# Queries and keys from the token-major product, transposed on TensorE, in place of three feature-major products

## The chip, the cores and the metric

The kernel runs on one core of a Trainium2 chip. The metric is the device time of one execution, in microseconds (us). The engines: TensorE (PE: matmuls and transposes, PEld its weight loads), VectorE (DVE), ScalarE (ACT), GpSimd (POOL), SyncE (SP, which issues DMAs).

## The reference

16 sequences ("groups") of 512 tokens with 128 features, fp32. Each is normalised; a causal linear attention with 32 channels and a decay, and a mixture of four experts with top-2 routing are computed of it and added to x.

```python
xn = _layernorm(x)
# attention, C = 32
q_w = basis @ q_coeffs.T                     # also k_w, v_w, o_w
queries, keys, values = xn @ q_w, xn @ k_w, xn @ v_w
scores = einsum('btc,bsc->bts', queries, keys)
diff = pos[None, :] - pos[:, None]
scores = scores * decay ** max(diff - 1, 0) * (diff > 0)
attn = (einsum('bts,bsc->btc', scores, values) @ o_w.T) * out_scale
# experts, top 2 of 4 by softmax of the logits
e0 = silu(xn @ w1) * (xn @ w3) @ w2
e1 = gelu(folded(xn) @ c1 + b) @ c2 + b
e2: syn -> attn -> layernorm -> relu FFN -> layernorm -> gen
e3 = gelu(xn @ ml_w1 + b) @ ml_w2 + b
out = x + attn + sum(weight * expert)
```

## The kernel before

**Products.** Most products are done as three float32r matmuls of high and low parts: high x high, low x high, high x low (`xh`, `xl` for the input, `WH`, `WL` for the weights). They are feature-major: weights stand, 512 tokens move, the result is features x tokens. The first product of a group, though, is token-major: for each of 4 tiles of 128 tokens, `xh`/`xl` stand and `TH`/`TL` move (lines 1146 to 1148). Its 196 columns are 128 for expert 2, 4 router logits, 32 of k and 32 of v.

**Order.** Everything is written out by hand, with semaphores. Each engine has a function `turn(g, first, last)`, called for group 0 and 1, for 2 to 13 in a loop over pairs, and for 14 and 15; a turn also holds leftovers of the group before. `UNITS` lists 24 products in the order in which TensorE fills the four PSUM banks `S0` to `S3` in turn: `tok0` to `tok3`, the first gate (`a0`, `b0`), four products of expert 3 (`c0` to `c3`), state (`st`), scores (`sc`), gate 1, and so on. A bank may be filled again when its reader has released it.

**A group on TensorE:** transposes of the last group's `u` into `ATT` (L1246); the token product; q and k, feature-major (L1155 to L1157) into `qk_bank`, which is `ATT` under another name and holds q, q, k, k in four times 32 partitions; gate 0 (`three`, L1133 to L1135); `c0` to `c3`; the state product of `kd` and `kv` (L1168); transposes of the normed `n1` (L1173); scores (L1179); gate 1; experts 1 and 2 of the group before; `pr` and `qd` into `ATT` (L1191, L1194); `f1`; attention's output (L1207 to L1209), which waits for `found_low`; gates 2 and 3; `e3`, `f2`, `m0`, `m1`, expert 0 (L1059).

**VectorE:** `u` statistics (L786); `pl` out of the token banks (L845), each behind the ScalarE copy of the same bank (`kv_taken`), which releases the bank; statistics; low part of Q (L856); gate 0's two products (L818, L822); low part of K (L861); expert 0's mixing; `qd` (L871), which is q, three times over on 96 partitions, times the decay table `reach`; `pr` (L811), the masked scores; `h2l` (L875); gate 1; expert 1's mixing; five routing steps; `foundl` (L716), the low part of what attention found; routing; and so on.

**ScalarE:** `kv` copies (L573); Q (L578: 96 partitions, q, q, k); tanh of gate 0 (L567); K twice (L580, L581); `kd` (L585); four Gelus out of `c0` to `c3` (L588), each releasing its bank; state (L590); `h2` (L592) and `h2h` (L595); tanh of gate 1; `hid3h`; `foundh` (L601).

**GpSimd** takes the roots and norms (`n1`, L454) and low parts of the hidden layers.

Setup folds weights: `qkv` is one product of 160 columns (q, q, k, k, v), which ScalarE and VectorE split into `WH`/`WL` (columns `qk`) and `TH`/`TL`.

Of the kernel before, what the change touches and what calls it, by code (L numbers as in the profile page):

```python
# [18 lines left out]
ALU = mybir.AluOpType  # L19
# [3 lines left out]
P = 128  # L23
GROUPS = 16
T = 512
NT = T // P
PAIRS = GROUPS // 2
C = 32
E = 4
I = 512  # L30
# [31 lines left out]
SPLIT, _at = {}, 0  # L62
for _name, _width in (("w1", I), ("w3", I), ("ml", I), ("f1", 2 * P), ("f2", 2 * P), ("w2", I), ("me", 2 * P), ("qk", 4 * C)):
    SPLIT[_name] = _at
    _at += _width
# [7 lines left out]
LOGW = P + E  # L73
TOKW = LOGW + 2 * C


B = 32
BEHIND = NT - 1
# [54 lines left out]
def build(nc: bass.Bass, x: bass.AP, weights: bass.AP, vecs: bass.AP, rows: bass.AP, out: bass.AP):  # L133
    with ExitStack() as ctx:
        def sb(name, shape, dt=F32):
            return ctx.enter_context(nc.sbuf_tensor(name, shape, dt))

        def sem(name):
            return ctx.enter_context(nc.semaphore(name))
# [19 lines left out]
        mask = sb("mask", [P, P])  # L159
        reach = sb("reach", [BEHIND * C, BEHIND * P])  # L160
        depth = sb("depth", [P, 2])
# [11 lines left out]
        xl = [sb(f"xl{k}", [P, T], F32R) for k in range(2)]  # L173
        kv = sb("kv", [P, NT, 2 * C])
        kd = sb("kd", [P, BEHIND, C])
# [88 lines left out]
        qk_ready = sem("qk_ready")  # L264
        qk_high = sem("qk_high")
        qk_split = sem("qk_split")
        kv_taken = sem("kv_taken")
# [81 lines left out]
        def _(sp):  # L349
# [20 lines left out]
            for n in range(BEHIND):  # L370
                sp.dma_start(reach[n * C:(n + 1) * C, :], bass.AP(source, start - (P - 1) - n * P,
                                                                  [diagonals.ap[0], [0, C], [1, BEHIND * P]])) \
                    .then_inc(mask_loaded, DMA_INC)
# [132 lines left out]
        def _(act):  # L506
# [14 lines left out]
            def high_weights(n):  # L521

                first_col, name, width = WEIGHT_SPLITS[n]
                act.wait_ge(w_loaded[LOAD_OF[name]], DMA_INC)
                src = w(name, 0, width)
                act.copy(WH[:, first_col:first_col + width], src).then_inc(split_high, 1)
# [13 lines left out]
            qkv = prod("qkv", cols=5 * C)  # L540
            at = SPLIT["qk"]
            act.copy(WH[:, at:at + 2 * C], qkv[:, 0:2 * C])
            act.copy(WH[:, at + 2 * C:at + 4 * C], qkv[:, C:3 * C])
            act.copy(TH[:, LOGW:TOKW], qkv[:, 3 * C:5 * C]).then_inc(fold_high, 1)
            act.copy(TH[:, 0:P], prod("ce")).then_inc(fold_high, 1)
# [13 lines left out]
            def turn(g, first, last):  # L559
# [11 lines left out]
                for t in range(NT):  # L571
                    tok, _ = unit(f"tok{t}")
                    act.copy(kv[:, t, :], tok[:, LOGW:TOKW]).then_inc(kv_taken, 1)  # L573
                if first:
                    for n in range(FIRST_SPLITS, len(WEIGHT_SPLITS)):
                        high_weights(n)
                act.wait_ge(qk_ready, g.count(1, 1))
                act.copy(Q[:, :], qk_bank[0:3 * C, :]).then_inc(qk_high, 1)  # L578
                half_gate(0)
                act.copy(K[0:C, :], qk_bank[3 * C:4 * C, :])  # L580
                act.copy(K[C:2 * C, :], qk_bank[3 * C:4 * C, :]).then_inc(qk_high, 1)  # L581
                if first:
                    act.wait_ge(depth_loaded, DMA_INC)
                act.wait_ge(kv_taken, g.count(NT, NT))
                act.mul(kd[:, :, :], kv[:, 1:NT, 0:C], depth[:, 0:1]).then_inc(kd_ready, 1)  # L585
                for j in range(4):
# [40 lines left out]
        def _(dve):  # L627
# [34 lines left out]
            n = 1  # L662
# [16 lines left out]
            def took(ins):  # L679

                ins.then_inc(setup_took, 1)
                dve.wait_ge(setup_took, taken[0])

            dve.tensor_tensor(tokb[:, P:P + E], row("router_b"), row("balancer"), ALU.add)
            product("qkv")
            qkv, at = prod("qkv", cols=5 * C), SPLIT["qk"]
            dve.wait_ge(fold_high, 1)
            dve.tensor_tensor(WL[:, at:at + 2 * C], qkv[:, 0:2 * C], WH[:, at:at + 2 * C], ALU.subtract)
            dve.tensor_tensor(WL[:, at + 2 * C:at + 4 * C], qkv[:, C:3 * C], WH[:, at + 2 * C:at + 4 * C], ALU.subtract)
            took(dve.tensor_tensor(TL[:, LOGW:TOKW], qkv[:, 3 * C:5 * C], TH[:, LOGW:TOKW], ALU.subtract))  # L690
            product("ce")
# [110 lines left out]
            def turn(g, first, last):  # L802
# [49 lines left out]
                for t in range(NT):  # L852
                    ins = dve.bn_aggr(mv["c"][:, t, :], stats["c"][:, t, :])
                ins.then_inc(c_stats, 1)
                dve.wait_ge(qk_high, g.count(2, 1))
                dve.tensor_tensor(Q[C:2 * C, :], qk_bank[C:2 * C, :], Q[C:2 * C, :], ALU.subtract)  # L856
                silu(0)
                if not first:
# [10 lines left out]
                if first:  # L869
                    dve.wait_ge(mask_loaded, (1 + BEHIND) * DMA_INC)  # L870
                dve.tensor_tensor(qd[:, :], qk_bank[0:BEHIND * C, 0:BEHIND * P], reach[:, :], ALU.mult) \  # L871
                    .then_inc(qd_ready, 1)
# [113 lines left out]
        def _(pe):  # L986
# [136 lines left out]
            def turn(g, first, last):  # L1123
# [26 lines left out]
                if first:  # L1150
                    fold_first()
                if not first:
                    pe.wait_ge(u_read, g.prev().count(1, 1))
                wh, wl = (m[:, SPLIT["qk"]:SPLIT["qk"] + 4 * C] for m in (WH, WL))
                pe.matmul(qk_bank, wh, h, start=True, stop=False)  # L1155
                pe.matmul(qk_bank, wh, l, start=False, stop=False)
                pe.matmul(qk_bank, wl, h, start=False, stop=True).then_inc(qk_ready, 1)  # L1157
                if first:
                    pe.wait_ge(split_low, 1)
                gates(0)  # L1160
                if first:
                    pe.wait_ge(split_low, 2)
# [4 lines left out]
                for n in range(BEHIND):  # L1167
                    ins = pe.matmul(bank[n * C:(n + 1) * C, 0:C], kd[:, n, :], kv[:, n + 1, C:2 * C],  # L1168
                                    start=True, stop=True)
# [20 lines left out]
                for t in range(NT):  # L1190
                    ins = pe.matmul(ATT[t * C:(t + 1) * C, 0, :], kv[:, t, C:2 * C], pr[:, t, :],  # L1191
                                    start=True, stop=(t == NT - 1))
# [121 lines left out]
```

## Time and profile before

| | |
|---|---|
| runs | 451.05, 451.26, 454.0 us; median 451.26 |
| span of the profiled execution | 449.1 us |
| TensorE | 438.6 us busy (98%) |
| VectorE | 402.5 us (90%) |
| ScalarE | 271.4 us (60%) |
| GpSimd | 245.8 us (55%) |
| TensorE clock | 1.00 in the periods looked at |

The profile is of one execution and gives its span, from the first to the last instruction; what lies around it is not in it. A busy share is an average over the span. In a timeline each row has start, duration, engine, line, operation and the tiles out<-in; a bracket at the end has the engine's idle time before it and what ended it. A matmul's record lasts longer than the step to the next one, since they are pipelined: the step between starts is what TensorE's time is made of.

### The profile page before, as it was taken

Reading aid. Unit: us, or ns where it says so; the run is one execution under the profiler, and the core shown is the slowest. Engines: PE = TensorE matmul, PEld = TensorE weight load, DVE = VectorE, ACT = ScalarE, POOL = GpSimd, SP = SyncE. Lnnn points to the kernel's source line nnn. Section 1 sums busy time; section 2 is a strip of 40 time slices with the busy share of each in tenths; the row PEclk is TensorE's granted clock in tenths of the full one; section 3 lists DMA queues with packets and bytes.
Section 4 is the critical chain, followed back from the end, with each engine's and each line's share of the span. In section 5 each row is a group of like instructions: output and inputs, shape, how many; then the busy total and the mean of one; then the engine's idle time right before and its main releaser. Section 6 shows DMA issues by size and latency. Waiting matters only on the chain.

```text
span 449.1 us, 9603 instructions
## 1 busy us (share of the span) xinstructions
PE 438.6 (98%) x2804; PEld 371.8 (83%) x2804; DVE 402.5 (90%) x1344; ACT 271.4 (60%) x535; POOL 245.8 (55%) x366
## 2 busy tenths in 40 slices
PE   4999999999999999999999999999999999999997
PEld 3778888788888888888888988888888888888886
DVE  4887989989899898989989899898989989898897
ACT  4965838557384764838556484755838566483841
POOL 3893727557273664727466272664727466372451
PEclk9999999999999999999999999999999999999999
DMA  7522123032130412223032130413123031220201
GB/s 261 38 72 72 25 63 78 26 93 47 51 70 23 105 35 70 47 70 70 23 93 47 55 62 23 113 27 89 27 70 70 23 99 41 58 58 16 58 0 48
DMA packets 86484, 27.18 MB, mean 61 GB/s; under 512 B 64993, under 2 KB 82113, under 8 KB 86465
## 3 DMA queue, kind: packets, MB, share of 16 engines
q1 hardware_dynamic: 86176, 26.94, 25.0%
q8 instruction: 9, 0.15, 0.1%
q14 instruction: 11, 0.08, 0.1%
q10 hardware_dynamic: 288, 0.01, 0.0%
HBM read 14.66 MB, written 12.06 MB: 60 GB/s over the span
## 4 chain that ended last, share of the span: by engine, by line
PE 94%; DVE 3%; DMA 1%; issue 0%; DVEq 0%; ACT 0%; SPq 0%
PE S L1133 14%; PE S L1135 13%; PE S L1134 13%; PE EX L1059 12%; PE EX L1079 6%; PE S L1223 3%; PE S L1218 3%; PE S L1219 3%; PE EX L1087 3%; PE TR L1173 2%; PE S L1231 2%; PE S L1230 2%; PE S L1229 2%; PE S L1148 2%; PE S L1147 2%; PE S L1146 2%
## 5 line engine op out<-in xcount | busy, mean ns | idle before, releaser
L486 POOL TENSOR_TENSOR hid3l<-hid,hid3h 128x512 fp32r<-128x512 f32 x64 | 80.3, 1287 | 29.3 <-ACT hid3h L599 29.3
L1133 PE MATMUL S<-xh,WH 128*128 128x512 f32 x224 | 90.4, 403 | 0.0
L1135 PE MATMUL S<-xh,WL 128*128 128x512 f32 x224 | 88.4, 394 | 0.0
L1134 PE MATMUL S<-xl,WH 128*128 128x512 f32 x224 | 88.1, 393 | 0.0
L444 POOL TENSOR_TENSOR veps_x<-mv_x,eps 128x4 f32<-128x4 f32 x16 | 3.2, 200 | 111.7 <-DVE mv_x L643 111.7
L1059 PEld LDWEIGHTS EX<-scaled,hid 128*128 128x128 f32 x480 | 55.9, 192 | 1.2
L1059 PE MATMUL EX<-scaled,hid 128*128 128x128 f32 x480 | 56.0, 275 | 0.0
L1133 PEld LDWEIGHTS S<-xh,WH 128*128 128x128 f32 x224 | 42.2, 188 | 14.1 <-DVE hid L822 3.1
L1135 PEld LDWEIGHTS S<-xh,WL 128*128 128x128 f32 x224 | 42.1, 188 | 9.9
L573 ACT COPY kv<-S 128x64 f32<-128x64 f32 x64 | 13.6, 213 | 60.3 <-PE S L1148 54.6
L1134 PEld LDWEIGHTS S<-xl,WH 128*128 128x128 f32 x224 | 42.3, 189 | 8.0
L822 DVE TENSOR_TENSOR hid<-gate,S 128x512 f32<-128x512 f32 x64 | 44.0, 688 | 4.2
L490 POOL TENSOR_TENSOR hidl<-hid,hidh 128x512 fp32r<-128x512 f32 x32 | 40.9, 1300 | 11.0 <-ACT hidh L609 11.0
L818 DVE SCALAR_TENSOR_TENSOR gate<-th,S 128x512 f32<-128x512 f32 x64 | 43.8, 684 | 1.8
L567 ACT ACTIVATE th<-S 128x512 f32<-128x512 f32 x64 | 38.1, 595 | 8.8 <-PE S L1135 6.9
L588 ACT ACTIVATE hid<-S,VEC 128x512 f32<-128x512 f32 x64 | 38.8, 690 | 0.4
L752 DVE SCALAR_TENSOR_TENSOR OUT<-EX,coef,OUT 128x128 f32<-128x128 f32 x124 | 34.8, 344 | 0.6 <-PE EX L1069 0.2
L599 ACT CAST hid3h<-hid 128x512 fp32r<-128x512 f32 x64 | 34.6, 615 | 0.0
L621 ACT ACTIVATE hid<-S,me_b 128x512 f32<-128x512 f32 x32 | 22.0, 687 | 19.2 <-PE S L1135 19.1
L519 ACT CAST xh<-TR 128x512 fp32r<-128x512 f32 x16 | 9.4, 588 | 37.6 <-DVE TR L800 37.4
L1079 PEld LDWEIGHTS EX<-W,hid 128*128 128x128 f32 x240 | 29.1, 191 | 1.3
L454 POOL TENSOR_SCALAR n<-pl,negmean_c,rstd_c 128x128 f32<-128x128 f32 x64 | 27.8, 451 | 2.8 <-issue 2.8
(201 smaller groups left out, 1066.4 us busy)
## 6 DMA issues: line engine op xcount, KB each, us to landing
X<-x SPq DMA_DIRECT2D x16, 256.0 KB, 2.8
turning<-xn SPq DMA_DIRECT2D x15, 256.0 KB, 2.6
xb<-turning SPq DMA_DIRECT2D x60, 64.0 KB, 2.6
turning<-e3T SPq DMA_DIRECT2D x15, 256.0 KB, 2.4
e3b<-turning SPq DMA_DIRECT2D x60, 64.0 KB, 2.6
out<-OUT SPq DMA_DIRECT2D x15, 256.0 KB, 2.4
W<-weights SPq DMA_DIRECT2D x1, 768.0 KB, 8.2
W<-weights SPq DMA_DIRECT2D x1, 512.0 KB, 5.8
```

The lines of the kernel that those rows point to most:

```text
L486: pool.tensor_tensor(hid3l[:, j, :], hid[3][:, j, :], hid3h[:, j, :], ALU.subtract) \
L490: pool.tensor_tensor(hidl[:, j, :], hid[2][:, j, :], hidh[:, j, :], ALU.subtract) \
L567: act.activation(th[:, j, :], a[:, :], ACT.Tanh, scale=0.5).then_inc(th_ready, 1)
L588: act.activation(hid[3][:, j, :], c[:, :], ACT.Gelu, bias=vec(f"ml_b1{j}")).then_inc(free, 1)
L752: ins = dve.scalar_tensor_tensor(out=OUT[g.par][:, t, :], in0=(src or EX[EX_BANK[e]])[:, t, :], scalar=coef[g.par][:, t, e:e + 1], in1=OUT ...
L818: dve.scalar_tensor_tensor(out=gate[:, j, :], in0=th[:, j, :], scalar=1.0, in1=a[:, :], op0=ALU.add, op1=ALU.mult).then_inc(a_free, 1)
L822: dve.tensor_tensor(hid[0][:, j, :], gate[:, j, :], b[:, :], ALU.mult).then_inc(b_free, 1)
L1059: ins = pe.matmul(EX[EX_BANK[0]][:, t, :], hid[0][:, j, t * P:(t + 1) * P], scaled[:, j * P:(j + 1) * P], start=(j == 0), stop=(j == 3))
L1079: ins = pe.matmul(EX[EX_BANK[1]][:, t, :], hid[1][:, j, t * P:(t + 1) * P], w("me_c2w", j * P, P), start=(j == 0), stop=(j == 1))
L1133: pe.matmul(bank[:, :], wh, hi, start=True, stop=False)
L1134: pe.matmul(bank[:, :], wh, lo, start=False, stop=False)
L1135: pe.matmul(bank[:, :], wl, hi, start=False, stop=True).then_inc(unit_ready, 1)
```

## The change

q and k come out of the token-major product as well. Its columns become 228: q, k and v, 32 each, behind the 132. ScalarE's copy takes all three and writes each twice, so that `kv[:, t]` has q, q, k, k, v, v (192 columns). TensorE transposes the first 128 of them, four tiles, into `qk_bank`, which then holds q, q, k, k on its partitions as before. The three feature-major matmuls and their weights in `WH`/`WL` go. On TensorE gate 0 stands in front of the transposes. On ScalarE the tanh of gate 0 stands in front, Q is copied for 64 partitions, K in one copy of 64, and the third part of Q is now q again, in a copy of its own (`q_again`). On VectorE gate 0 stands ahead of the low part of Q, and `qd` is two instructions, on 64 and on 32 partitions, as `qk_bank` has q only twice; `reach` is split likewise. Lines of the changed kernel are 2 to 6 further down.

```diff
-for ... ("me", 2 * P), ("qk", 4 * C)):
+for ... ("me", 2 * P)):
-TOKW = LOGW + 2 * C
+TOKW = LOGW + 3 * C
-        reach = sb("reach", [BEHIND * C, BEHIND * P])
+        reach = sb("reach", [2 * C, BEHIND * P])
+        reach_far = sb("reach_far", [C, BEHIND * P])
-        kv = sb("kv", [P, NT, 2 * C])
+        kv = sb("kv", [P, NT, 3, 2, C])
...
# ScalarE, setup
-            act.copy(WH[:, at:at + 2 * C], qkv[:, 0:2 * C])
-            act.copy(WH[:, at + 2 * C:at + 4 * C], qkv[:, C:3 * C])
-            act.copy(TH[:, LOGW:TOKW], qkv[:, 3 * C:5 * C]).then_inc(fold_high, 1)
+            act.copy(TH[:, LOGW:LOGW + 2 * C], qkv[:, C:3 * C])
+            act.copy(TH[:, LOGW + 2 * C:TOKW], qkv[:, 4 * C:5 * C]).then_inc(fold_high, 1)
# ScalarE, turn
-                    act.copy(kv[:, t, :], tok[:, LOGW:TOKW]).then_inc(kv_taken, 1)
+                    both = tok[:, LOGW:TOKW].rearrange("p (a c) -> p a c", a=3).unsqueeze(2).broadcast_to([P, 3, 2, C])
+                    act.copy(kv[:, t, :, :, :], both).then_inc(kv_taken, 1)
...
+                half_gate(0)
                 act.wait_ge(qk_ready, g.count(1, 1))
-                act.copy(Q[:, :], qk_bank[0:3 * C, :]).then_inc(qk_high, 1)
-                half_gate(0)
-                act.copy(K[0:C, :], qk_bank[3 * C:4 * C, :])
-                act.copy(K[C:2 * C, :], qk_bank[3 * C:4 * C, :]).then_inc(qk_high, 1)
+                act.copy(Q[0:2 * C, :], qk_bank[0:2 * C, :]).then_inc(qk_high, 1)
+                act.copy(K[0:2 * C, :], qk_bank[2 * C:4 * C, :]).then_inc(qk_high, 1)
+                act.copy(Q[2 * C:3 * C, :], qk_bank[0:C, :]).then_inc(q_again, 1)
# VectorE, turn
+                silu(0)
                 dve.wait_ge(qk_high, g.count(2, 1))
                 dve.tensor_tensor(Q[C:2 * C, :], qk_bank[C:2 * C, :], Q[C:2 * C, :], ALU.subtract)
-                silu(0)
...
-                dve.tensor_tensor(qd[:, :], qk_bank[0:BEHIND * C, 0:BEHIND * P], reach[:, :], ALU.mult) \
+                dve.wait_ge(q_again, g.count(1, 1))
+                dve.tensor_tensor(qd[0:2 * C, :], qk_bank[0:2 * C, 0:BEHIND * P], reach[:, :], ALU.mult)
+                dve.tensor_tensor(qd[2 * C:3 * C, :], qk_bank[0:C, 0:BEHIND * P], reach_far[:, :], ALU.mult) \
                     .then_inc(qd_ready, 1)
# TensorE, turn
+                gates(0)
                 if not first:
                     pe.wait_ge(u_read, g.prev().count(1, 1))
-                wh, wl = (m[:, SPLIT["qk"]:SPLIT["qk"] + 4 * C] for m in (WH, WL))
-                pe.matmul(qk_bank, wh, h, start=True, stop=False)
-                pe.matmul(qk_bank, wh, l, start=False, stop=False)
-                pe.matmul(qk_bank, wl, h, start=False, stop=True).then_inc(qk_ready, 1)
-                gates(0)
+                for t in range(NT):
+                    pe.wait_ge(kv_taken, g.count(NT, t + 1))
+                    ins = pe.transpose(qk_bank[:, t * P:(t + 1) * P],
+                                       kv[:, t, 0:2, :, :].rearrange("p a b c -> p (a b c)"), ident[:, :])
+                ins.then_inc(qk_ready, 1)
...
                 pe.wait_ge(qk_split, g.count(1, 1))
+                pe.wait_ge(q_again, g.count(1, 1))
```

On TensorE, at the start of group 1, before, from the last matmul of the token product to the first of `c0` (`S` are the four banks):

```order
L1148 MATMUL S<-TH,xl 128x196
L1155 MATMUL ATT<-xh,WH 128x512 [waits u_read]
L1156 MATMUL ATT<-xl,WH 128x512
L1157 MATMUL ATT<-xh,WL 128x512
L1133 MATMUL S<-xh,WH 128x512 [waits released0]
L1134 MATMUL S<-xl,WH 128x512
L1135 MATMUL S<-xh,WL 128x512
L1133 MATMUL S<-xh,WH 128x512 [waits released1]
L1134 MATMUL S<-xl,WH 128x512
L1135 MATMUL S<-xh,WL 128x512
L1133 MATMUL S<-xh,WH 128x512 [waits released2]
```

The same place after:

```order
L1152 MATMUL S<-TH,xl 128x228
L1137 MATMUL S<-xh,WH 128x512 [waits released0]
L1138 MATMUL S<-xl,WH 128x512
L1139 MATMUL S<-xh,WL 128x512
L1137 MATMUL S<-xh,WH 128x512 [waits released1]
L1138 MATMUL S<-xl,WH 128x512
L1139 MATMUL S<-xh,WL 128x512
L1163 MATMUL ATT<-ident,kv 128x128 [waits kv_taken,u_read]
L1163 MATMUL ATT<-ident,kv 128x128 [waits kv_taken] x3
L1137 MATMUL S<-xh,WH 128x512 [waits released2]
```

Gate 0 has moved directly behind the token product, and four transposes stand behind it, in front of `c0`.

On VectorE in the same group, before, from the statistics of `pl` to the low part of `h2`:

```order
L853 BN_AGGR mv_c<-stats_c 128x2 x4
L856 TENSOR_TENSOR Q<-ATT,Q 32x512 [waits qk_high]
L818 SCALAR_TENSOR_TENSOR gate<-th,S 128x512 [waits th_ready]
L822 TENSOR_TENSOR hid<-gate,S 128x512 [waits released0,unit_ready]
L792 BN_AGGR mv_u<-stats_u 128x2 x4
L861 TENSOR_TENSOR K<-ATT,K 32x512 [waits qk_high]
...
L871 TENSOR_TENSOR qd<-ATT,reach 96x384
L811 TENSOR_TENSOR pr<-S,mask 128x512 [waits unit_ready]
L875 TENSOR_TENSOR h2l<-h,h2h 128x512 [waits h2_high]
```

The same place after:

```order
L855 BN_AGGR mv_c<-stats_c 128x2 x4
L820 SCALAR_TENSOR_TENSOR gate<-th,S 128x512 [waits th_ready]
L824 TENSOR_TENSOR hid<-gate,S 128x512 [waits released0,unit_ready]
L859 TENSOR_TENSOR Q<-ATT,Q 32x512 [waits qk_high]
L794 BN_AGGR mv_u<-stats_u 128x2 x4
L863 TENSOR_TENSOR K<-ATT,K 32x512 [waits qk_high]
...
L874 TENSOR_TENSOR qd<-ATT,reach 64x384 [waits q_again]
L875 TENSOR_TENSOR qd<-ATT,reach_far 32x384
L813 TENSOR_TENSOR pr<-S,mask 128x512 [waits unit_ready]
L879 TENSOR_TENSOR h2l<-h,h2h 128x512 [waits h2_high]
```

The gate's two instructions have moved ahead of the low part of Q, and `qd` has become two.

## Rows read from the trace of the kernel before

**Rows 1.** The page: span; engines' busy time, share and instructions.

```profile
span 449.1 us, 9603 instructions
PE 438.6 (98%) x2804; PEld 371.8 (83%) x2804; DVE 402.5 (90%) x1344; ACT 271.4 (60%) x535; POOL 245.8 (55%) x366
```

**Rows 2.** Busy time by engine in one period: PE, PEld, DVE, ACT, POOL; TensorE clock.

```profile
200.64:227.47 26.83, 26.83 (x174) 22.73 (x173) 24.68 (x82) 16.46 (x32) 14.94 (x23) 1.00 0.24 58
```

**Rows 3.** Timeline of TensorE, 202 to 228: start, duration, engine, line, operation.

```profile
202.40 0.42 PE L1155 MATMUL ATT<-xh,WH 128*128 128x512 f32 x1
...
203.13 0.40 PE L1133 MATMUL S<-xh,WH 128*128 128x512 f32 x1
...
205.91 0.43 PE L1133 MATMUL S<-xh,WH 128*128 128x512 f32 x1
...
207.64 0.66 PE L1173 MATMUL TR<-ident,n 128*128 128x128 f32 x4
...
223.90 3.73 PE L1059 MATMUL EX<-scaled,hid 128*128 128x128 f32 x32
227.47 0.60 PE L1246 MATMUL ATT<-ident,u 128*128 128x128 f32 x4
```

**Rows 4.** Timeline of VectorE, 202 to 229.

```profile
202.09 0.28 DVE L845 TENSOR_TENSOR pl<-S,tokb 128x132 f32<-128x132 f32 x1
...
202.85 0.29 DVE L845 TENSOR_TENSOR pl<-S,tokb 128x132 f32<-128x132 f32 x1
...
204.41 0.68 DVE L856 TENSOR_TENSOR Q<-ATT,Q 32x512 fp32r<-32x512 f32 x1
205.10 0.69 DVE L818 SCALAR_TENSOR_TENSOR gate<-th,S 128x512 f32<-128x512 f32 x1
...
208.78 0.54 DVE L871 TENSOR_TENSOR qd<-ATT,reach 96x384 f32<-96x384 f32 x1
209.25 0.68 DVE L811 TENSOR_TENSOR pr<-S,mask 128x512 f32<-128x512 f32 x1
210.09 0.69 DVE L875 TENSOR_TENSOR h2l<-h,h2h 128x512 fp32r<-128x512 f32 x1 [0.17 <-ACT h2h L595]
...
214.31 0.29 DVE L716 TENSOR_TENSOR foundl<-ATT,foundh 128x128 fp32r<-128x128 f32 x1
...
228.11 0.89 DVE L786 BATCH_NORM_STATS2 stats_u<-ATT 128x6 f32<-128x128 f32 x4 [0.94 <-PE ATT L1246]
```

**Rows 5.** TensorE's matmuls and weight loads (PEld) at 214.6.

```profile
214.58 0.39 PE L1135 MATMUL S<-h2h,WL 128*128 128x512 f32 x1
214.82 0.39 PE L1207 MATMUL ATT<-backh,foundh 128*128 128x512 f32 x1
...
214.65 0.19 PEld L1207 LDWEIGHTS ATT<-backh,foundh 128*128 128x128 f32 x1
```

**Rows 6.** Group 0: VectorE and TensorE at the attention's output.

```profile
26.51 0.28 DVE L716 TENSOR_TENSOR foundl<-ATT,foundh 128x128 fp32r<-128x128 f32 x1
...
26.94 0.47 PE L1207 MATMUL ATT<-backh,foundh 128*128 128x512 f32 x1 [0.26 <-DVE foundl L716]
```

**Rows 7.** The transposes of `n`: durations (ns) min/median/max, first and last start.

```profile
L1173 PE MATMUL TR<-ident,n x64: 272/273/329, 20.6 to 422.8; 128*128 128x128 f32 x64
```

**Rows 8.** Timeline of ScalarE, 202 to 214.

```profile
202.60 0.21 ACT L573 COPY kv<-S 128x64 f32<-128x64 f32 x1
...
204.64 0.58 ACT L580 CAST K<-ATT 32x512 fp32r<-32x512 f32 x1
...
205.84 0.38 ACT L585 ACTIVATE kd<-kv,depth 128x96 f32<-128x96 f32 x1
206.24 2.43 ACT L588 ACTIVATE hid<-S,VEC 128x512 f32<-128x512 f32 x4
...
209.44 0.62 ACT L595 CAST h2h<-h 128x512 fp32r<-128x512 f32 x1
...
213.44 0.27 ACT L601 CAST foundh<-ATT 128x128 fp32r<-128x128 f32 x1 [0.82 <-PE ATT L1194]
```

More of the change, by code:

```diff
@@ L62 @@
 SPLIT, _at = {}, 0
-for _name, _width in (("w1", I), ("w3", I), ("ml", I), ("f1", 2 * P), ("f2", 2 * P), ("w2", I), ("me", 2 * P), ("qk", 4 * C)):
+for _name, _width in (("w1", I), ("w3", I), ("ml", I), ("f1", 2 * P), ("f2", 2 * P), ("w2", I), ("me", 2 * P)):
     SPLIT[_name] = _at
@@ L265, in build @@
         qk_high = sem("qk_high")
+        q_again = sem("q_again")
         qk_split = sem("qk_split")
@@ L370, in _ @@
             for n in range(BEHIND):
-                sp.dma_start(reach[n * C:(n + 1) * C, :], bass.AP(source, start - (P - 1) - n * P,
-                                                                  [diagonals.ap[0], [0, C], [1, BEHIND * P]])) \
+                to = reach[n * C:(n + 1) * C, :] if n < 2 else reach_far[:, :]
+                sp.dma_start(to, bass.AP(source, start - (P - 1) - n * P,
+                                          [diagonals.ap[0], [0, C], [1, BEHIND * P]])) \
                     .then_inc(mask_loaded, DMA_INC)
@@ L540, in _ @@
             qkv = prod("qkv", cols=5 * C)
-            at = SPLIT["qk"]
-            act.copy(WH[:, at:at + 2 * C], qkv[:, 0:2 * C])
-            act.copy(WH[:, at + 2 * C:at + 4 * C], qkv[:, C:3 * C])
-            act.copy(TH[:, LOGW:TOKW], qkv[:, 3 * C:5 * C]).then_inc(fold_high, 1)
+            act.copy(TH[:, LOGW:LOGW + 2 * C], qkv[:, C:3 * C])
+            act.copy(TH[:, LOGW + 2 * C:TOKW], qkv[:, 4 * C:5 * C]).then_inc(fold_high, 1)
             act.copy(TH[:, 0:P], prod("ce")).then_inc(fold_high, 1)
@@ L584, in turn @@
                 act.wait_ge(kv_taken, g.count(NT, NT))
-                act.mul(kd[:, :, :], kv[:, 1:NT, 0:C], depth[:, 0:1]).then_inc(kd_ready, 1)
+                act.mul(kd[:, :, :], kv[:, 1:NT, 1, 0, :], depth[:, 0:1]).then_inc(kd_ready, 1)
                 for j in range(4):
@@ L685, in _ @@
             product("qkv")
-            qkv, at = prod("qkv", cols=5 * C), SPLIT["qk"]
+            qkv = prod("qkv", cols=5 * C)
             dve.wait_ge(fold_high, 1)
-            dve.tensor_tensor(WL[:, at:at + 2 * C], qkv[:, 0:2 * C], WH[:, at:at + 2 * C], ALU.subtract)
-            dve.tensor_tensor(WL[:, at + 2 * C:at + 4 * C], qkv[:, C:3 * C], WH[:, at + 2 * C:at + 4 * C], ALU.subtract)
-            took(dve.tensor_tensor(TL[:, LOGW:TOKW], qkv[:, 3 * C:5 * C], TH[:, LOGW:TOKW], ALU.subtract))
+            dve.tensor_tensor(TL[:, LOGW:LOGW + 2 * C], qkv[:, C:3 * C], TH[:, LOGW:LOGW + 2 * C], ALU.subtract)
+            took(dve.tensor_tensor(TL[:, LOGW + 2 * C:TOKW], qkv[:, 4 * C:5 * C], TH[:, LOGW + 2 * C:TOKW],
+                                   ALU.subtract))
             product("ce")
@@ L1151, in turn @@
                     fold_first()
-                if not first:
-                    pe.wait_ge(u_read, g.prev().count(1, 1))
-                wh, wl = (m[:, SPLIT["qk"]:SPLIT["qk"] + 4 * C] for m in (WH, WL))
-                pe.matmul(qk_bank, wh, h, start=True, stop=False)
-                pe.matmul(qk_bank, wh, l, start=False, stop=False)
-                pe.matmul(qk_bank, wl, h, start=False, stop=True).then_inc(qk_ready, 1)
                 if first:
@@ L1160, in turn @@
                 gates(0)
+                if not first:
+                    pe.wait_ge(u_read, g.prev().count(1, 1))
+                for t in range(NT):
[3 more added lines that the diff above has]
+                ins.then_inc(qk_ready, 1)
                 if first:
@@ L1167, in turn @@
                 for n in range(BEHIND):
-                    ins = pe.matmul(bank[n * C:(n + 1) * C, 0:C], kd[:, n, :], kv[:, n + 1, C:2 * C],
+                    ins = pe.matmul(bank[n * C:(n + 1) * C, 0:C], kd[:, n, :], kv[:, n + 1, 2, 0, :],
                                     start=True, stop=True)
@@ L1190, in turn @@
                 for t in range(NT):
-                    ins = pe.matmul(ATT[t * C:(t + 1) * C, 0, :], kv[:, t, C:2 * C], pr[:, t, :],
+                    ins = pe.matmul(ATT[t * C:(t + 1) * C, 0, :], kv[:, t, 2, 0, :], pr[:, t, :],
                                     start=True, stop=(t == NT - 1))
```

## The prediction

> **What bounds the kernel now.** I read the page first: TensorE is busy 98% of the span, VectorE 90% [rows 1]. The reader should not stop there, since a record that is busy says nothing of whether it could have started earlier. So I took one period, the stretch from one group's transposes of `u` (200.64) to the next one's (227.47): 26.83 us, no idleness on TensorE, its clock at 1.00 [rows 2]. Then I read each engine's timeline in it. The three feature-major matmuls of q and k take TensorE from 202.40 to 203.13, so 0.24 us each; the twelve that start from 203.13 on, up to 205.91, take 0.232 each [rows 3]. VectorE stands idle for 0.94 us until the `u` transposes are done, and from there to `foundl` it has one gap, 0.17 us, where `h2l` waits for ScalarE's `h2h` [rows 4]. `foundl` ends at 214.31 + 0.29 = 214.60. The weights of the matmul that waits for it are loaded at 214.65, a little behind the start of the matmul before it (214.58), which is where a load starts that waits for nothing; the matmul itself still starts on time at 214.82 [rows 5]. How much could be spared there is seen in group 0, where TensorE did stand idle for `foundl`: it ended at 26.51 + 0.28 = 26.79, the matmul started at 26.94, 0.15 us later [rows 6]. In the steady group 214.60 + 0.15 = 214.75, so the slack ahead of 214.82 is 0.07 us. So two chains make one period: VectorE with ScalarE from the end of the `u` transposes to `foundl`, and TensorE from there to the end of the next `u` transposes. What lengthens the first by more than 0.07 us is paid in every group, whatever TensorE saves in the meantime.
>
> **TensorE's own account.** Three matmuls of 512 columns go: 203.13 - 202.40 = 0.73 us [rows 3]. Four transposes of 128x128 come. The nearest are those of `n`: the record of four lasts 0.66 from 207.64, each one 0.27 [rows 3, 7], so the last starts 0.39 behind the first; with its own pitch of 0.13 at most that is 0.52, and with the 0.11 that 128 columns take elsewhere ((227.47 - 223.90) / 32 [rows 3]) 0.44. I take 0.44, as most rows have it. The token product goes from 196 to 228 columns, twelve times. Below: 228 columns at the rate of 512 would take 0.232 x 228 / 512 = 0.10, less than the 0.11 that 128 columns take anyway, so nothing. Above: by a line from 128 columns (0.11) to 512 (0.232), 32 x 0.00032 = 0.010 each, 0.12 in all. I take 0.04, near the flat end. TensorE's work shrinks by 0.73 - 0.44 - 0.04 = 0.25 us a group, 4.0 us over 16.
>
> The Trainium skill, "TensorE: Matmul & The Clock Gate", section on PE-mode transpose, gives about 275 ns for a 128x128 transpose in a kernel's context, mostly access latency. By that number as the cost of each in a row, four would take 1.1 us, and the 0.25 saved would be 0.41 lost. The trace has the same duration and decides against that reading: each record lasts 273 ns [rows 7], and they start 0.13 us apart with the clock at 1.00 [rows 2, 3].
>
> **VectorE's part.** (a) The `kv` copy writes 192 columns instead of 64. The fourth starts at 202.60 and lasts 0.21 [rows 8]; the fourth `pl` starts 0.04 behind its end, at 202.85 [rows 4]: VectorE waits for it. For 192 columns the bounds are 0.21 (if only what is read counts) and 0.62 (the 512 columns of `h2h`). `foundh`, 128 columns out of PSUM, takes 0.27, so 64 more columns cost 0.06 [rows 8]; twice that gives 0.33, I take 0.32. `pl` and all behind it come 0.11 + 0.04 (the token product) = 0.15 later. (b) The gate comes ahead of the Q subtraction: three instructions in another order, nothing. (c) `qd` becomes two instructions of 384 columns. If cost went by partitions this would be free (end: 0). But the Q subtraction on 32 partitions takes 0.68, `pr` on 128 partitions 0.68 [rows 4]. So each costs what the one did, from `qd` at 208.78 to `pr` at 209.25: 0.47 more. VectorE is free for `h2l` 0.62 later, less the 0.17 of idleness: 0.45.
>
> **ScalarE's part.** Q, tanh, K, K, `kd` becomes tanh, Q, K, Q again, `kd`, but Q now waits for transposes that stand behind the first gate. The first gate's matmul waits for the first `pl`, 202.09 + 0.28 = 202.37; from a release to the matmul it is 0.12 (gate ends 205.10 + 0.69 = 205.79, matmul at 205.91) [rows 3, 4]: 202.49. Six matmuls at 0.232: 203.88. From the first transpose's start to the last's 0.39, its record 0.27, a semaphore's 0.04: Q starts at 204.58. Three copies at 0.60 (K at 204.64, two of them, `kd` at 205.84) and `kd` 0.40: the first Gelu at 206.78 instead of 206.24 [rows 8]. From the Gelus ScalarE runs without a gap to the end of `h2h` (209.44 + 0.62), which so comes 0.54 later. That is more than VectorE's 0.45 and decides: `h2l`, and `foundl` with it, 0.54 late; less the slack of 0.07, TensorE's matmul on `foundh` starts 0.47 late.
>
> **Where TensorE's saving goes.** Queued behind the new waits on TensorE are the state product, the scores and gate 1; they need the banks of the first three Gelus, which come 0.54 late, so the 0.25 saved is waited away there, inside the 0.47 and not on top of it. Behind `foundl` TensorE runs on as before. VectorE, 0.54 late, still has its 0.94 us ahead of the next `u` statistics [rows 4], so nothing is added and nothing recovered.
>
> **The sum.** 15 groups x 0.47 = 7.05 us. In group 0 VectorE is the later one already (0.26 us of idleness at `foundl` [rows 6]), so the second `qd` counts in full: 0.5. Setup loses some copies and subtractions of 64 columns ahead of the first group; at most 0.2 us, and the wider `kv` copies of group 0 take it back: nothing. Its DMAs are as many as before, and SP's queue is the same. Span 449.1 [rows 1] + 7.5 = 456.6. The profile gives no other time of its execution than the span; the median of the runs, 451.26, stands 2.2 above it: 458.8 us, 1.7% more.
>
> **Rivals.** *TensorE's work decides.* For it: 98% busy. Against it: the 0.07 of slack. It needs a second `qd` at next to nothing and a ScalarE order that fits, so that `foundl` comes less than 0.07 late. It gives -4.0: 447.3, and with the flat ends (token product free) 446.6. 0.11, of it 0.05 faster by over 1%.
> *Only the second `qd` counts.* ScalarE is early enough, since Q's copy on fewer partitions is short, and the `kv` copy stays at 0.21: 0.47 + 0.04 - 0.17 - 0.07 = 0.27 a group, and 0.2 if the pitch is shorter; 3 to 4 us, 454.8, within 1%. 0.10.
> *The wide `kv` copy is dear.* It writes in four dimensions; `kd` in three blocks takes 0.38 for 96 columns [rows 8], so 0.46 may be true for 192. Then the four copies run one behind the other from 201.59 (three pitches of 0.34 ahead of 202.60), the last ends at 203.43 instead of 202.81, VectorE is at `h2l` 0.62 + 0.47 - 0.17 = 0.92 late: 0.85 a group, 13 us, 464. 0.08.
> *Transposes at their full 0.27 in a row.* 0.7 later through Q, Gelu and `h2h`: 1.1 a group, 17 us, 468. 0.03.
> The forecast has 0.68.
>
> **From this to the numbers.** A measurement of this kernel tells about 1% from no change. Slower by over 1%: 0.68 + 0.08 + 0.03 = 0.79; within: 0.10 + 0.06 = 0.16; faster: 0.05. The range goes down to 450, so that it holds the second rival and leaves out the first, and up to 463, for a copy somewhat dearer than 0.32; the forecast's own is 455.5 to 462 (0.28 to 0.7 a group).
>
> **What will show it.** Right, step by step: two `qd` of 0.54; `kv` copies near 0.32; the first Gelu 6.1 us behind the `u` transposes' start (206.78 less 200.64) and `h2l` waiting for `h2h`; the weights of the matmul on `foundh` 0.4 us behind the start of the matmul ahead, or TensorE idle for `foundl`; a period of 27.3 us with VectorE's wait for the `u` transposes still near 0.9. Wrong: a period under 26.9; a `kv` copy over 0.4; q and k transposes that start over 0.2 us apart; TensorE's longest wait at another matmul than that on `foundh`.

## The result, and the profile after

The changed kernel takes 456.86 us (median of 4 runs), the kernel before 451.15 beside it: a ratio of 1.0119, interval 1.0087 to 1.0151. The forecast was slower, 458.8 us in a range of 450 to 463; measured are +5.7 us instead of +7.5.

One thing on the kernels has to be put right first. The description ahead of the prediction says that `qk_bank` holds q, q, k, k before the change too, and that the copy on 96 partitions is q, q, k. In fact it holds q, q, q, k before, and the copy is q three times over; q, q, k, k is the changed kernel's order, which is why it needs a further copy of q and a second `qd`. No number of the prediction rests on this.

The page of the changed kernel (busy time, share, instructions), where TensorE is still busy 97%, answers to [rows 1]:

```profile
span 454.4 us, 9652 instructions
PE 440.7 (97%) x2820; PEld 372.0 (82%) x2820; DVE 409.2 (90%) x1359; ACT 276.6 (61%) x534; POOL 246.7 (54%) x366
```

The same period as in [rows 2], from one group's `u` transposes to the next (busy time of PE, PEld, DVE, ACT, POOL; clock):

```profile
202.82:229.99 27.17, 27.02 (x176) 22.78 (x174) 25.09 (x83) 16.77 (x32) 14.96 (x23) 1.00 0.24 57
```

27.17 us instead of 26.83, at the same clock. 0.34 in 15 groups is 5.1 of the 5.3 us by which the span grew. To compare instants with those before, take 2.18 us off: the `u` statistics start at 203.46 here and at 201.28 there.

TensorE's timeline, answering to [rows 3] and [rows 5]:

```profile
202.82 0.60 PE L1252 MATMUL ATT<-ident,u 128*128 128x128 f32 x4
...
203.37 0.28 PE L1151 MATMUL S<-TL,xh 128*128 128x228 f32 x1
...
204.48 0.28 PE L1152 MATMUL S<-TH,xl 128*128 128x228 f32 x1
204.60 0.50 PE L1137 MATMUL S<-xh,WH 128*128 128x512 f32 x1
...
206.11 0.60 PE L1163 MATMUL ATT<-ident,kv 128*128 128x128 f32 x4
206.46 0.48 PE L1137 MATMUL S<-xh,WH 128*128 128x512 f32 x1
...
216.87 0.40 PE L1139 MATMUL S<-h2h,WL 128*128 128x512 f32 x1
217.23 0.50 PE L1213 MATMUL ATT<-backh,foundh 128*128 128x512 f32 x1
217.57 0.40 PE L1214 MATMUL ATT<-backh,foundl 128*128 128x512 f32 x1
```

The work on TensorE did shrink: the four transposes take 0.35 us (206.11 to 206.46) and the 228 columns the same 0.11 as 196 (203.37 to 204.48 for ten steps). But between the matmul at 216.87 and the second of the attention's output (L1214) at 217.57 lie 0.70 us for two matmuls that took 0.47 before (214.58 to 215.05). VectorE's timeline says why, answering to [rows 4]:

```profile
203.46 0.89 DVE L788 BATCH_NORM_STATS2 stats_u<-ATT 128x6 f32<-128x128 f32 x4 [1.07 <-PE ATT L1252]
204.27 1.18 DVE L847 TENSOR_TENSOR pl<-S,tokb 128x132 f32<-128x132 f32 x4
...
206.30 0.38 DVE L855 BATCH_NORM_AGGREGATE mv_c<-stats_c 128x2 f32<-128x6 f32 x4
206.59 0.66 DVE L820 SCALAR_TENSOR_TENSOR gate<-th,S 128x512 f32<-128x512 f32 x1
...
210.94 0.54 DVE L874 TENSOR_TENSOR qd<-ATT,reach 64x384 f32<-64x384 f32 x1
211.49 0.55 DVE L875 TENSOR_TENSOR qd<-ATT,reach_far 32x384 f32<-32x384 f32 x1
212.07 0.69 DVE L813 TENSOR_TENSOR pr<-S,mask 128x512 f32<-128x512 f32 x1
212.68 0.68 DVE L879 TENSOR_TENSOR h2l<-h,h2h 128x512 fp32r<-128x512 f32 x1
...
216.88 0.29 DVE L718 TENSOR_TENSOR foundl<-ATT,foundh 128x128 fp32r<-128x128 f32 x1
```

`h2l` is 0.41 later than before (212.68 - 2.18 - 210.09), `foundl` 0.39. ScalarE, answering to [rows 8]:

```profile
206.74 0.58 ACT L581 CAST Q<-ATT 64x512 fp32r<-64x512 f32 x1 [0.54 <-PE ATT L1163]
207.35 0.59 ACT L582 CAST K<-ATT 64x512 fp32r<-64x512 f32 x1
207.96 0.57 ACT L583 CAST Q<-ATT 32x512 fp32r<-32x512 f32 x1
208.56 0.38 ACT L587 ACTIVATE kd<-kv,depth 128x96 f32<-128x96 f32 x1
208.84 2.41 ACT L590 ACTIVATE hid<-S,VEC 128x512 f32<-128x512 f32 x4
...
212.01 0.62 ACT L597 CAST h2h<-h 128x512 fp32r<-128x512 f32 x1
```

`h2h` ends at 212.63, VectorE comes out of `pr` at the same time, and `h2l` starts at 212.68 with no idleness: two engines arrive together. The waits (total, times, longest) have a line that they did not have before:

```profile
DVE stats_u L788 <- PE ATT L1252: 18.4, 15, 2.4
...
PEld ATT L1213 <- DVE foundl L718: 6.5, 15, 0.6
```

The weights of the matmul on `foundh` wait 0.43 us for `foundl` in each of 15 groups. In the program the one wait for `foundl` stands ahead of all three matmuls of that output, though only the second reads it; no run moved the wait. VectorE still idles ahead of the `u` statistics, 1.07 us, so it is not VectorE's total that is short: it is a chain of VectorE's and ScalarE's instructions from the `u` transposes to `foundl`.

### The profile page after: what moved, and what is told of

Its sections match the earlier page's. It is cut to its first block, busy times and chain, and to the rows that moved or that the text cites. A ratio compares the mean times of both kernels' runs of the same rounds, so it can differ in the third digit from the quotient of the medians.

```text
span 454.4 us, 9652 instructions
## 1 busy us (share of the span) xinstructions
PE 440.7 (97%) x2820; PEld 372.0 (82%) x2820; DVE 409.2 (90%) x1359; ACT 276.6 (61%) x534; POOL 246.7 (54%) x366
## 3 DMA queue, kind: packets, MB, share of 16 engines
q1 hardware_dynamic: 86176, 26.94, 24.7%
## 4 chain that ended last, share of the span: by engine, by line
PE 77%; DVE 10%; issue 5%; ACT 5%; DMA 1%; DVEq 1%; SPq 0%; ACTq 0%
PE EX L1063 12%; PE S L1137 10%; PE S L1138 9%; PE S L1139 9%; PE EX L1083 5%; PE S L1229 3%; PE S L1224 3%; PE S L1225 3%; PE EX L1091 2%; PE TR L1178 2%; DVE OUT L754 2%; PE ATT L1213 2%; PE S L1235 2%; PE S L1236 2%; PE S L1237 2%
## 5 line engine op out<-in xcount | busy, mean ns | idle before, releaser
L1137 PE MATMUL S<-xh,WH 128*128 128x512 f32 x224 | 92.4, 413 | 0.0
L575 ACT COPY kv<-S 128x192 f32<-128x192 f32 x64 | 20.4, 320 | 55.5 <-PE S L1152 54.8
L568 ACT ACTIVATE th<-S 128x512 f32<-128x512 f32 x64 | 38.2, 596 | 18.4 <-PE S L1139 18.4
L788 DVE BATCH_NORM_STATS2 stats_u<-ATT 128x6 f32<-128x128 f32 x64 | 14.3, 286 | 18.4 <-PE ATT L1252 18.4
```

Of the source, the lines that this page charges most:

```text
L1137: pe.matmul(bank[:, :], wh, hi, start=True, stop=False)
```

## The experiments

Two theories were open. A: that chain sets the period, and of its two halves (VectorE's, ScalarE's) the later one counts; besides it GpSimd's norm of `n` holds up gate 1. Against it: one edit alone is the cost (second `qd`, ScalarE's third copy, the order), or TensorE's work is.

**One instruction for `qd`.** The last third of `qd` is then k times the decay, so the far part of attention is left out.

```diff
-                dve.tensor_tensor(qd[0:2 * C, :], qk_bank[0:2 * C, 0:BEHIND * P], reach[:, :], ALU.mult)
-                dve.tensor_tensor(qd[2 * C:3 * C, :], qk_bank[0:C, 0:BEHIND * P], reach_far[:, :], ALU.mult) \
+                dve.tensor_tensor(qd[:, :], qk_bank[0:BEHIND * C, 0:BEHIND * P], reach[:, :], ALU.mult) \
```

> The changed kernel with qd as one instruction on 96 partitions (its last third is then k times the decay, so the attention's far part is not computed). Theory A (the chain from the u transposes over VectorE and ScalarE to foundl sets the period; in the changed kernel h2l starts at 212.68 both because VectorE is just free and because h2h has just ended): VectorE comes 0.66 us earlier to h2l but waits there for ScalarE; no gain, 455.5 to 457 us. Rival B (the second qd on VectorE is the whole cost): back to 451.5 us. Rival C (TensorE's own work costs): 456.9 us, with no new wait of VectorE at h2l.

Measured: 455.64 us, ratio 1.0097 (1.0069 to 1.0126). The waits of this run:

```profile
DVE h2l L877 <- ACT h2h L596: 8.7, 16, 0.6
PEld ATT L1211 <- DVE foundl L717: 6.5, 15, 0.5
```

VectorE saved 0.6 us a group and stood idle nearly as long for `h2h` (8.7 us in 16 waits); TensorE's wait for `foundl` is still 6.5 us. The period hardly moved: 27.16 (`u` statistics at 202.79 and 229.95). Of what it is below the changed kernel, about half lies ahead of the loop: the first `u` statistics start at 39.87 us in this trace and at 40.44 in the changed kernel's. Rival B falls.

**One instruction for Q.** The last third of Q is k, so one of the three terms of the scores is another one.

```diff
-                act.copy(Q[0:2 * C, :], qk_bank[0:2 * C, :]).then_inc(qk_high, 1)
+                act.copy(Q[:, :], qk_bank[0:3 * C, :]).then_inc(qk_high, 1)
-                act.copy(Q[2 * C:3 * C, :], qk_bank[0:C, :]).then_inc(q_again, 1)
```

> The changed kernel with Q copied in one ScalarE instruction on 96 partitions and no copy of q again (Q's last third is then k, so one term of the scores is not computed rightly). Theory A: ScalarE has h2h 0.6 us earlier, but VectorE is only free for h2l at the same time as now; no gain, 455.5 to 457 us. Rival D (ScalarE's order and third copy are the whole cost): -0.34 us a group, 451.5 us.

Measured: 457.43 us, ratio 1.0111 (1.0061 to 1.0160): no gain. Rival D falls too.

**Both.**

> Both edits together. Theory A: h2l and foundl come about 0.6 us earlier, TensorE no longer waits for foundl (0.23 us a group), but gate 1 stays where it is, since the last transpose of n waits for GpSimd's norm: 452 to 454 us. Rival E (TensorE's work sets the period once foundl is out of the way): 26.83 - 0.25 us a group, 447 us. Rivals B or D alone: the same as the one of the two single edits.

Measured: 451.68 us, ratio 1.0007 (0.9985 to 1.0029), 5.2 us below the changed kernel where the single edits gave 1.2 and nothing. By the periods, 4.1 of it comes from the loop (15 x 0.27). The sum of two edits that are worth nothing alone is the mark of two chains that end together. `foundl` is gone from the waits (but for group 0), and in its place stands GpSimd:

```profile
PEld TR L1173 <- POOL n L455: 4.3, 15, 0.3
```

The period is 26.90 (`u` statistics at 202.76 and 229.66), not the 26.58 that TensorE's work alone would give: rival E falls. The time itself was 0.3 below what theory A had given.

**The order back**, in the changed kernel: transposes ahead of gate 0 on TensorE, Q ahead of the tanh, low part of Q ahead of the gate.

```diff
+                for t in range(NT):
+                    pe.wait_ge(kv_taken, g.count(NT, t + 1))
...
                 gates(0)
-                for t in range(NT):
-                    pe.wait_ge(kv_taken, g.count(NT, t + 1))
```

> The changed kernel with the transposes of q and k in front of gate 0 again, on TensorE, ScalarE (Q ahead of the tanh) and VectorE (low part of Q ahead of the gate). Theory A: TensorE waits about 0.4 us for the last kv copy, ScalarE reaches the Gelus 0.5 us earlier, VectorE 0.13 later since the low part of Q stands in front of the gate; VectorE decides: 458 us (457 to 459). Rival F (gate first is what costs, by holding up Q on ScalarE): 451 to 453 us.

Measured: 458.89 us, ratio 1.0146 (1.0099 to 1.0192). On TensorE the transposes take 0.66 us (207.21 to 207.87) instead of 0.35, since the last waits for its `kv` copy:

```profile
207.21 0.90 PE L1160 MATMUL ATT<-ident,kv 128*128 128x128 f32 x4
207.87 0.49 PE L1137 MATMUL S<-xh,WH 128*128 128x512 f32 x1
...
207.78 0.14 PEld L1160 LDWEIGHTS ATT<-ident,kv 128*128 128x128 f32 x1 [0.19 <-ACT kv L575]
```

TensorE's wait for `foundl` grew from 6.5 to 7.9 us in all. Gate 0 in front does not cost here, it saves 2 us; 1.7 of them are the period, 27.28 instead of 27.17 in the middle groups.

**The order alone**, in the kernel before: gate 0 ahead of the three feature-major products, on all three engines.

```diff
+                gates(0)
                 pe.matmul(qk_bank, wh, h, start=True, stop=False)
                 pe.matmul(qk_bank, wh, l, start=False, stop=False)
                 pe.matmul(qk_bank, wl, h, start=False, stop=True).then_inc(qk_ready, 1)
-                gates(0)
```

> The kernel before with gate 0 in front of the three feature-major products, on TensorE, ScalarE and VectorE: the order alone. Theory A: Q's copy starts 1.4 us later and the tanh falls out between, so the first Gelu comes 0.7 to 0.8 us later, and with it h2h, h2l and foundl; less 0.07 of slack 0.65 a group: 460 to 462 us. Rival (the order is free, as GpSimd and TensorE have other limits): 450 to 452 us.

Measured: 461.79 us, ratio 1.0239 (1.0218 to 1.0261), with `h2l` waiting up to 1.0 us for ScalarE:

```profile
DVE h2l L875 <- ACT h2h L595: 15.6, 16, 1.0
```

The same order that saves 2 us in the changed kernel costs 10.6 in this one, where the products wait for no `kv` copy and Q is just later.

**Two instructions for `qd`**, in the kernel before, nothing else.

```diff
-                dve.tensor_tensor(qd[:, :], qk_bank[0:BEHIND * C, 0:BEHIND * P], reach[:, :], ALU.mult) \
+                dve.tensor_tensor(qd[0:2 * C, :], qk_bank[0:2 * C, 0:BEHIND * P], reach[0:2 * C, :], ALU.mult)
+                dve.tensor_tensor(qd[2 * C:3 * C, :], qk_bank[2 * C:3 * C, 0:BEHIND * P], reach[2 * C:3 * C, :], ALU.mult) \
```

> The kernel before with qd as two instructions, on 64 and on 32 partitions, nothing else: VectorE 0.66 us more up to pr (0.55 + 0.58 instead of 0.47, as in the changed kernel), less 0.17 of idleness and 0.07 of slack: 0.42 a group, 457 to 458 us. Rival (VectorE's 90% leave room for 0.5 us a group): 451 us.

Measured: 457.01 us, ratio 1.0126 (1.0109 to 1.0143). VectorE's timeline:

```profile
211.71 0.54 DVE L871 TENSOR_TENSOR qd<-ATT,reach 64x384 f32<-64x384 f32 x1
212.27 0.56 DVE L872 TENSOR_TENSOR qd<-ATT,reach 32x384 f32<-32x384 f32 x1
212.85 0.69 DVE L811 TENSOR_TENSOR pr<-S,mask 128x512 f32<-128x512 f32 x1
```

1.14 us from `qd` to `pr` instead of 0.47, and a period of 27.17 in the middle groups, the changed kernel's. This one instruction costs as much as the whole change.

**One product of three**, in the kernel before. The two products with low parts are left out, 0.47 us a group of TensorE's work, more than the change took.

```diff
-                pe.matmul(qk_bank, wh, h, start=True, stop=False)
-                pe.matmul(qk_bank, wh, l, start=False, stop=False)
-                pe.matmul(qk_bank, wl, h, start=False, stop=True).then_inc(qk_ready, 1)
+                pe.matmul(qk_bank, wh, h, start=True, stop=True).then_inc(qk_ready, 1)
```

> The kernel before with only the first of the three feature-major products of q and k (the low parts are left out): TensorE has 0.47 us a group less to do, more than the change took off it. Theory A: nothing of it reaches the period, since the last transpose of n waits for GpSimd's norm and foundl has 0.07 of slack: 450 to 451.2 us, TensorE's wait shows ahead of the transposes of n. Rival E (TensorE's work sets the time): 16 x 0.47 = 7.5 us less, 443.6 us.

Measured: 451.31 us, ratio 1.0011 (0.9993 to 1.0029). An engine that is busy 98% had 7.5 us taken off and the time did not move, not even by the little that theory A allowed. The idleness showed, but not where the expectation had it: the products `c2` waited for VectorE's gate.

```profile
PEld S L1133 <- DVE gate L818: 10.3, 16, 0.7
```

The longest was 0.2 in the kernel before. The first line here is the second matmul of `c2` in the kernel before (the first is the one at 205.91 [rows 3]); the others are the `u` transposes and the first two matmuls of `c2` in this run:

```profile
206.18 0.39 PE L1134 MATMUL S<-xl,WH 128*128 128x512 f32 x1
...
200.50 0.60 PE L1244 MATMUL ATT<-ident,u 128*128 128x128 f32 x4
...
205.71 0.50 PE L1133 MATMUL S<-xh,WH 128*128 128x512 f32 x1 [0.23 <-DVE gate L818]
206.04 0.39 PE L1134 MATMUL S<-xl,WH 128*128 128x512 f32 x1
```

From the `u` transposes to `c2`'s second matmul it is 5.54 us in both (206.18 - 200.64, 206.04 - 200.50). So in the kernel before `c2` was already held by gate 0, which ended at 205.79: it lost 0.04 there (205.91 to 206.18 is 0.27, not 0.23), while the matmuls around `foundl` kept their step of 0.23. GpSimd's norm of `n` is as tight:

```profile
206.13 1.74 POOL L454 TENSOR_SCALAR n<-pl,negmean_c,rstd_c 128x128 f32<-128x128 f32 x4 [0.17 <-issue]
...
207.64 0.42 PEld L1173 LDWEIGHTS TR<-ident,n 128*128 128x128 f32 x4
```

It ends at 207.87, and the last of the four loads, of 0.14, starts 0.05 later. Both hang on the same `pl` and statistics of VectorE.

**The wide `kv` copy**, in the kernel before: k and v written three times each.

```diff
-                    act.copy(kv[:, t, :], tok[:, LOGW:TOKW]).then_inc(kv_taken, 1)
+                    wide = tok[:, LOGW:TOKW].rearrange("p (a c) -> p a c", a=2).unsqueeze(2).broadcast_to([P, 2, 3, C])
+                    act.copy(kv[:, t, :, :, :], wide).then_inc(kv_taken, 1)
```

> The kernel before with the kv copy written three times over (192 columns, 0.32 us as in the changed kernel), nothing else. VectorE's fourth pl, the statistics and GpSimd's norm come 0.11 us later. Theory A: the h2l side hides it in its 0.17 us of idleness, the last transpose of n does not: 0.05 to 0.11 us a group, 452 to 453 us. Rival (a copy on an engine that is 60% busy costs nothing): 451.2 us.

Measured: 452.96 us, ratio 1.0040 (1.0022 to 1.0057); its period is 26.94 (`u` statistics at 201.82 and 228.76), 0.11 longer. 0.11 us of a copy, on an engine 60% busy, goes into the period in full, through `pl` and the statistics. The wait that grew is not the one that was expected. It is `c2`'s for gate 0; in the kernel before it was the second line:

```profile
PEld S L1134 <- DVE gate L819: 4.7, 15, 0.3
...
PEld S L1133 <- DVE gate L818: 3.1, 15, 0.2
```

GpSimd's norm comes 0.10 later as well and is again followed by the last load at once, so which of the two holds the period is not separated here.

**Moves that should cure it.** First `foundl` alone, from behind the fifth routing step to behind the second, in the changed kernel.

```diff
                 route(dve.tensor_tensor(same, other, mine, ALU.is_equal))
+                if not first:
+                    found_rest(g)
...
-                if not first:
-                    found_rest(g)
                 route(dve.tensor_reduce(rank, same, AX.X, ALU.add))
```

> The changed kernel with foundl moved up on VectorE, from behind the fifth routing step to behind the second (0.8 us earlier). Theory A: TensorE no longer waits for foundl (0.23 us a group); gate 1 stays bound by GpSimd's norm, which the wide kv copy has put 0.11 us later, so the period is 26.93: 453 us (452 to 454), like the two relieved edits together. Rival (a second wait takes its place behind foundl, or VectorE's later work moves with it): 455 to 457 us.

Measured: 453.59 us, ratio 1.0062 (1.0037 to 1.0086), period 26.89 (202.31 to 229.20), as expected. An instruction of 0.29 us, moved, gives back 3.3 of the 5.7 us. The period is that of the run with both edits (26.90), though the times differ by 1.9 us: what lies ahead of the loop differs from trace to trace, and the first `u` statistics start anywhere from 39.9 to 42.4 us in the fourteen.

Then also half of expert 1's products in front of the state product, for both kernels:

```diff
+                if not first:
+                    expert1(g.prev(), 0)    # tiles 0 and 1
                 pe.wait_ge(kd_ready, g.count(1, 1))
...
-                    expert1(g.prev())
+                    expert1(g.prev(), 1)    # tiles 2 and 3
```

> The same, and on TensorE half of expert 1's products of the group before (0.9 us) stand ahead of the state product and the transposes of n, as cover for GpSimd's norm. Theory A: both waits are covered now, and TensorE's own account decides at last: 26.33 to 26.6 us a group, 444 to 448 us. Rival (moving c_turned back moves h2, h2h and h2l back by as much, and the wait reappears at f1 or foundl): 451 to 453 us.

> The kernel before with the same two moves (foundl up, half of expert 1 ahead of the transposes of n). Theory A: TensorE's own account here is 26.58 to 26.75 us a group: 447 to 450 us, and 2 to 4 us above the changed kernel with the same moves, since the 0.25 us of TensorE that the change saves counts now. Rival: no gain, as both versions have another wait: 451 us, and the changed one not faster than it.

Measured: 453.64 us (1.0050; 1.0032 to 1.0067) for the changed kernel: no further gain. 455.68 us (1.0105; 1.0080 to 1.0130) for the one before, which is worse than without the moves. In the changed one TensorE now runs through to gate 3 without waiting, and then waits for VectorE's gate 2, which frees the bank of `e3`:

```profile
PEld S L1228 <- DVE gate L820: 7.2, 15, 0.6
```

The expectation's rival named the wrong place, theory A the wrong time. For the kernel before, the rival was right in its first half, no gain; the changed kernel is 2.0 us faster than it with the same moves, as theory A had it. TensorE waits at the same place there, 6.8 us, and the transposes of `n` come too late for ScalarE, so that `h2l` waits:

```profile
PEld S L1222 <- DVE gate L818: 6.8, 15, 0.5
...
ACT h L592 <- PE TR L1177: 5.8, 15, 0.4
DVE h2l L875 <- ACT h2h L595: 5.6, 15, 0.4
```

Last, the scaling of expert 2 (1.1 us on VectorE) also moved from ahead of gate 2 to behind it, in the changed kernel.

```diff
-                if not first:
-                    expert2_scale(g.prev())
...
                 silu(2)
+                if not first:
+                    expert2_scale(g.prev())
```

> The changed kernel with foundl up, half of expert 1 ahead of the transposes of n, and on VectorE the four instructions that scale expert 2 (1.1 us) moved from ahead of gate 2 to behind it. In the run with the first two moves TensorE's idleness had gone to the product e3, whose bank gate 2 frees (7.2 us in 15 waits, up to 0.6). Theory A (chain after chain in a stream on VectorE that is nearly full, each to be put behind what TensorE waits for): this wait goes too, the period is 26.4 to 26.65 us, 446 to 449 us, below both kernels. Rival (VectorE itself is now the bound, at about 25.7 us of work and 0.8 of wait for the u transposes a group, and yet another wait appears): 451 to 454 us.

Measured: 451.36 us, ratio 1.0003 (0.9981 to 1.0024). The wait for gate 2 is gone. The `u` transposes at 200.75 and 227.35 are 26.60 apart, but the periods on either side are 27.03 and 27.02, and the mean of 14 is 26.78 (26.84 in the kernel before):

```profile
DVE stats_u L788 <- PE ATT L1256: 3.5, 2, 2.4
...
PE S L1139 <- DVE pl L847: 1.6, 5, 0.6
```

VectorE's wait for the `u` transposes, 18.4 us in 15 groups in the changed kernel, is down to 3.5 in 2, and TensorE waits for `pl` instead. VectorE has hardly any reserve left, and gate 0, which the change put directly behind the token product, needs its `pl` first. The rival of this expectation was right. No version beat the kernel before.

## Why the prediction was right, and where its sizes were off

**The bound.** Right for the changed kernel: `foundl` sets its period, and not TensorE's work, as the run with `foundl` moved and the run with both edits show. Right also that TensorE's work does not set the time of the kernel before, which the run with one product of three shows. But what held that kernel was not `foundl`, which still had its slack. It was VectorE's gate 0 at `c2`, or GpSimd's norm just behind it. The prediction counted neither. It was lucky in that: the change itself puts gate 0 ahead of the low part of Q, so that it ends 0.72 earlier (206.59 + 0.66 - 2.18 = 205.07 instead of 205.79) and no longer counts, and the norm, 0.13 late, costs less than `foundl` does.

**TensorE's saving.** The prediction had 0.25 us a group. Its terms were off both ways: four transposes took 0.35 and not 0.44, and the wider token product nothing, but gate 0's first matmul, now directly behind that product, waits for the first `pl` (204.27 + 0.28, weights from 204.60). From the `u` transposes to the first matmul of `c0` it was 3.87 (204.51 - 200.64) and is 3.64 (206.46 - 202.82): 0.23 saved. At the state product nothing is left of it: 6.81 and 6.83 behind the `u` transposes.

```profile
204.51 0.40 PE L1133 MATMUL S<-xh,WH 128*128 128x512 f32 x1
...
207.45 0.26 PE L1168 MATMUL S<-kv,kd 128*32 128x32 f32 x6
...
209.65 0.26 PE L1173 MATMUL S<-kv,kd 128*32 128x32 f32 x6
```

It is worth nothing, as forecast. The rival with 0.27 us for each transpose in a row is out: each record of L1163 lasts 0.27, but the four and the next matmul start within 0.35.

**The `kv` copy.** Estimated 0.32, measured:

```profile
L575 ACT COPY kv<-S x64: 318/319/321, 13.7 to 422.2; 128x192 f32<-128x192 f32 x64
```

`pl` ends 0.13 late, the prediction had 0.15.

**The second `qd`.** Estimated 0.47, measured 1.13 - 0.47 = 0.66. The estimate took the step of an instruction that overlaps with the next; here neither the second `qd` nor `pr` starts before the one ahead has ended.

**The order on VectorE.** Estimated nothing, measured 0.13 to the good: from the aggregation to the Q subtraction it was 0.42 (203.99 to 204.41), from the aggregation to the gate it is 0.29. With the two errors against each other VectorE came out of `pr` almost as computed, by luck: 0.58 late (212.68 - 2.18, against 210.09 - 0.17), 0.41 with the old idleness of 0.17 taken off; the estimate was 0.45.

**ScalarE's term was mis-sized**, and it is the one that the sum rested on. Q started at 206.74 - 2.18 = 204.56 (204.58 computed), the three copies took 1.82 (1.80). But from `kd` to the first Gelu it was 0.28 and not 0.40, so the Gelus came 0.42 late and not 0.54, and `foundl` 0.39. Less the slack of 0.07 that is 0.32, and the period grew by 0.34; the prediction had 0.47. 0.13 in 15 groups are 2.0 us, nearly all of the 2.2 by which the span's growth of 5.3 fell short of the 7.5 forecast. The prediction said that ScalarE decides by 0.09; in the trace both engines arrive together, which the two single edits and their sum show.

**Group 0 and setup.** The prediction gave 0.5 for group 0 and nothing for setup. In group 0 TensorE idled 0.84 us at `pr` where it was 0.17, but the first `kv` copy started at 13.7 instead of 14.3, and the first `u` statistics at 40.4 instead of 40.3: 0.1 in all. How much of the earlier start is the change's and how much the first load's (TensorE's wait for weights was 5.8 instead of 6.0) was not taken apart.

## What to carry to other kernels

A share of 98% for an engine does not make its work the bound: look for the matmuls whose weights load later than the matmul ahead of them starts, and follow each of these chains back over the other engines, since several can be tight at once; taking work off the busiest engine is worth nothing until that chain is shorter. An edit that saves on the busiest engine by adding copies and small instructions elsewhere is to be priced on that chain, each instruction at its full length. When two engines arrive at the same time, undoing one edit shows nothing, so undo both before calling either harmless; and when one wait is cured, expect the next one close behind it, since a stream 90% full leaves little to move into.

## What the runs showed of the hardware

In these traces an instruction on VectorE that writes from another partition on than the one ahead starts only when that one has ended. `qd` on partitions 64 to 95 starts 0.55 and 0.56 behind a `qd` of 0.54, and `pr`, back on partition 0, 0.58 behind that; a `qd` on partitions 0 to 95 lets `pr` start after 0.47. The Q subtraction, written to partition 32, starts 0.42 behind the aggregation, the gate, written to partition 0, 0.29. The Trainium skill, "VectorE: DVE Perf Modes", section "Two Vector instructions with no wait between them", says that an instruction is held until all before it have finished when an input starts in another quadrant (a group of 32 partitions) than the last read from the same memory, or its output in another than the last write. By that rule, the trace agrees: the first `qd` gives way after 0.55 instead of 0.47, and the 0.58 from the second to `pr` makes the 0.66.

ScalarE seems to do the same, which was not expected. In six of the fourteen traces the last PSUM read ahead of `kd` starts at partition 0 (the changed kernel, its versions with one `qd`, with the order back and with the moves), and the Gelu starts 0.28 behind `kd` in every group. In the other eight it starts at partition 64 or 96 (all versions of the kernel before, one Q, both edits), and there it is 0.39 to 0.41. The nearest to a test are one Q and both edits: they take the last copy, from partition 0, out of the changed kernel, and 0.28 becomes 0.40. That the partition is the cause was not tested by itself.
